# Graph attention layer: softmax denominators summed per node by matmuls instead of scanned per edge

## The reference

```
h = layernorm(feat);  fh, ft, fe = h @ W_head.T, h @ W_tail.T, h @ W_ent.T
e = einsum(leaky_relu(fh[src] * ft[dst]), attn) * log(deg)[dst] / 16     # one score per edge and head
ex = exp(e - segment_max(e, dst)[dst])
a = ex / segment_sum(ex, dst)[dst]
f = fe
for _ in range(5):
    f = 0.85 * segment_sum(f[src] * a, dst) + 0.15 * fe
```

## Time and profile before

| what | us |
|---|---|
| median of 3 runs | 7686.8 |
| lowest and highest run | 7684.38, 7687.97 |
| span of the profiled execution, first to last instruction | 6856.9 |
| median less span | 829.9 |
| VectorE alone on the softmax, 1444.5 to 1646.4 | 201.9 |
| hop 0, first matmul to last (1678.7 to 1985.3) | 306.6 |

### The profile page before, as it was taken

The page is one execution under the profiler, slowest core; times in us unless marked ns, Lnnn a source line. Parts: engine busy times, 40 slices in busy tenths (PEclk is TensorE's granted clock), DMA queues, the critical chain, the costliest instruction groups (busy, mean ns, idle before and its releaser), DMA issues.

```text
span 6856.9 us, 96632 instructions
## 1 busy us (share of the span) xinstructions
PE 4373.3 (64%) x19868; PEld 3745.1 (55%) x19869; DVE 3934.0 (57%) x8770; ACT 406.8 (6%) x1393; POOL 4142.0 (60%) x4109
## 2 busy tenths in 40 slices
PE   2754554632778888876666655666654666664899
PEld 1443443521668888865555544555543555543899
DVE  5764655677876666626666645666644666654211
ACT  0111111110000000000000000000000000001100
POOL 1477775721027777767777776777776777774000
PEclk9655555555985555555555555555555555555999
DMA  1344464511642222222222222222222222232576
GB/s 40 104 141 123 143 154 125 148 54 56 180 133 75 76 75 75 76 56 74 76 75 75 75 61 71 75 75 76 75 68 65 76 75 76 75 73 79 185 271 233
DMA packets 540070, 671.65 MB, mean 98 GB/s; under 512 B 102862, under 2 KB 425131, under 8 KB 529996
## 3 DMA queue, kind: packets, MB, share of 16 engines
q0 software_dynamic: 143584, 320.73, 17.3%
q1 hardware_dynamic: 396444, 350.42, 16.6%
HBM read 511.17 MB, written 160.80 MB: 98 GB/s over the span
## 4 chain that ended last, share of the span: by engine, by line
POOL 45%; issue 32%; PE 10%; DVE 7%; DMA 4%; SPq 2%; POOLq 0%; ACT 0%; DVEq 0%; ACTq 0%; PEldq 0%; PEld 0%
POOL U L676 45%; PE ps L1081 6%; DMA U<-edge_fe 2%; PE ps L868 1%; DVE U L1488 1%; DVE U L1460 1%; DVE U L1185 1%; SPq L542 1%; DVE U L1101 1%; DVE U L1504 1%; PE ps L944 1%; SPq L583 0%; DMA U<-tab_f,stage 0%; DVE U L1272 0%; PE ps L930 0%
## 5 line engine op out<-in xcount | busy, mean ns | idle before, releaser
L676 POOL DMA_INDIRECT U<-tab_f,stage x3224 | 3215.9, 997 | 1368.1 <-issue 979.4
L868 PE MATMUL ps<-U 128*125 128x128 f32 x8160 | 2126.4, 418 | 1277.6 <-DVE U L1185 1276.2
L868 PEld LDWEIGHTS ps<-U 128*125 128x125 f32 x8160 | 1725.3, 300 | 1489.6 <-issue 1489.6
L1125 DVE TENSOR_TENSOR U<-dloc,iota_p 128x500 f32<-128x500 f32 x1225 | 840.0, 686 | 1606.4 <-DMA U<-tab_f,stage 1541.7
L676 POOL DMA_INDIRECT U<-tab_he,stage x806 | 849.9, 1054 | 470.8 <-issue 239.0
L856 PE MATMUL ps<-gap 128*128 128x125 f32 x2816 | 828.1, 448 | 117.3 <-DVE gap L1148 64.6
L856 PEld LDWEIGHTS ps<-gap 128*128 128x128 f32 x2816 | 661.7, 325 | 276.6 <-DVE gap L1148 273.3
L1185 DVE TENSOR_TENSOR U<-U,ex_it 128x512 f32<-128x512 f32 x1020 | 705.6, 692 | 0.0
L969 PE MATMUL ps<-U 125*128 x1632 | 422.3, 440 | 215.7 <-ACT U L776 215.7
L865 PEld LDWEIGHTS ps<-w_it,U 128*125 128x125 f32 x1632 | 435.7, 327 | 213.0 <-issue 213.0
L1160 DVE SCALAR_TENSOR_TENSOR gap<-gap,U,ps 128x125 f32<-128x125 f32 x1408 | 483.8, 344 | 108.5 <-DVE gap L1160 18.3
(11 more groups left out here) (238 smaller groups left out, 2478.8 us busy)
## 6 DMA issues: line engine op xcount, KB each, us to landing
adj<-gap SPq DMA_DIRECT2D x1408, 64.0 KB
edge_fe<-U SPq DMA_DIRECT2D x204, 256.0 KB, 2.5
U<-edge_fe SPq DMA_DIRECT2D x204, 256.0 KB, 2.9
U<-tab_f,stage POOLq DMA_INDIRECT x3224, 2.6
ex_it<-adj SPq DMA_DIRECT2D x30, 1600.0 KB, 6.2
U<-adj SPq DMA_DIRECT2D x30, 1600.0 KB, 6.1
fe_a<-adj SPq DMA_DIRECT2D x15, 1600.0 KB, 6.2
U<-tab_he,stage POOLq DMA_INDIRECT x806, 3.1
```

The source lines that it names most:

```text
L676: pool.indirect_dma_start(to[:, k, j, :], None, table, bass.IndirectOffsetOnAxis(ap=stage[:, k, j:j + 1], axis=0)).then_inc(got[k], 16)
L868: mm = nc.tensor.matmul(ps[0:BN, bass.ds(b * F, F)], hot[:, k, j, :], ga[:, k, j, :], start=False, stop=False, skip_group_check=True)
L1125: return v.tensor_tensor(to[:, (k + ahead) % SLOTS], dloc[:, bass.ds(item_of(r, k, ahead), G)].unsqueeze(2).to_broadcast([P, G, BN]), iota ...
```

## The change

The exponentials are no longer divided edge by edge. The two summing scans, the mask, the reciprocals and the scaling of all edges go away; `ex_it` holds bare exponentials, and the transposes wait for `exps_ready` of the three parts. In hop 0 each item gets a second matmul with the same one-hot weight and 8 moving columns (`ex_it` of the item), which adds the exponentials of a node and head in PSUM behind the other sums (`EXP_SUMS`). At the end of hop 0 VectorE makes `share` = 0.85 / sum per node and head (200 values to a partition), every eviction of every hop multiplies the bank by `share`, in hop 0 followed by an add of `fe_a`; `fe_a` is then divided by `share` once, and in hops 1 to 4 TensorE starts each cleared bank with `ident` times that `fe_a`, seven more matmuls a hop, so that the eviction needs no add.

```diff
-SCANS = 4
+SCANS = 2
...
                         for j, b in enumerate(buckets):
+                            if s == 0:
+                                nc.tensor.matmul(ps[0:BN, bass.ds(b * HEADS + EXP_SUMS, HEADS)], hot[:, k, j, :],
+                                                 ex_it[:, bass.ds(r * PER_ITER + (k * G + j), 1), :].rearrange("p i h -> p (i h)"),
+                                                 start=False, stop=False, skip_group_check=True)
...
-                pe.wait_ge(shares_ready, -(-min(CI, (n + 1) * BPB) * EXP_PARTS // CI))
+                pe.wait_ge(exps_ready, -(-min(CI, (n + 1) * BPB) * EXP_PARTS // CI))
...
                 clear(range(BANKS))
+                if n:
+                    pe.wait_ge(share_ready, 1)
+                    for k in range(BANKS):
+                        b0, b1 = bank_buckets(k)
+                        nc.tensor.matmul(bank(k, (b1 - b0) * F)[0:BN], ident[0:BN, 0:BN],
+                                         fe_a[0:BN, b0:b1, :].rearrange("p b f -> p (b f)"),
+                                         start=False, stop=False, skip_group_check=True)
                 sum_pass(n)
...
-            link(v.tensor_scalar(bw, gap[:, 0:L], 0.0, None, ALU.is_equal))
-            dve.wait_ge(exps_ready, EXP_PARTS)
-
-            scan_carried(2, fw, bw, e_sc, fw[:, L - 1:L], False, summing=True)
-            scan_carried(3, bw[:, ::-1], gap[:, 1:L + 1][:, ::-1], fw[:, ::-1], bw[:, 0:1], True)
-            for part_ in parts:
-                link(v.reciprocal(bw[:, part_], bw[:, part_]))
-                v.scalar_tensor_tensor(out=e_sc[:, part_], in0=e_sc[:, part_], scalar=1.0 - ALPHA, in1=bw[:, part_],
-                                       op0=ALU.mult, op1=ALU.mult).then_inc(shares_ready, 1)
...
+                if n == 0:
+
+                    share_ = share[0:BN].rearrange("p b h -> p (b h)")
+                    link(v.tensor_scalar(share_, ps[0:BN, EXP_SUMS:EXP_SUMS + NB * HEADS], 1.0, None, ALU.max))
+                    link(v.reciprocal(share_, share_))
+                    link(v.tensor_scalar(share_, share_, 1.0 - ALPHA, None, ALU.mult))
                 for k in range(BANKS):
                     b0, b1 = bank_buckets(k)
-                    v.tensor_tensor(na[0:BN, b0:b1], bank(k, (b1 - b0) * F)[0:BN].rearrange("p (b f) -> p b f", f=F),
-                                    fe_a[0:BN, b0:b1], ALU.add).then_inc(sums_out, 1)
+                    to = na[0:BN, b0:b1].rearrange("p b (h d) -> p (b h) d", h=HEADS)
+                    ins = v.tensor_tensor(to, bank(k, (b1 - b0) * F)[0:BN].rearrange("p (n d) -> p n d", d=HD),
+                                          over_heads(b0, b1), ALU.mult)
+                    if n == 0:
+                        link(ins)
+                        ins = v.tensor_tensor(na[0:BN, b0:b1], na[0:BN, b0:b1], fe_a[0:BN, b0:b1], ALU.add)
+                    ins.then_inc(sums_out, 1)
                 dve.wait_ge(sums_out, (n + 1) * BANKS)
+                if n == 0:
+
+                    link(v.reciprocal(back[0:BN], share[0:BN].rearrange("p b h -> p (b h)")))
+                    fe_ = fe_a[0:BN].rearrange("p b (h d) -> p (b h) d", h=HEADS)
+                    v.tensor_tensor(fe_, fe_, back[0:BN].unsqueeze(2).to_broadcast([BN, NB * HEADS, HD]),
+                                    ALU.mult).then_inc(share_ready, 1)
```

More of the change, by code:

```diff
@@ L94 @@
 W_SUMS = (NB + 1) * F
+EXP_SUMS = (NB + 1) * F
 MASKS = 9
 assert PER_ITER == CHUNKS and ITEMS % CHUNKS == 0 and CHUNKS * HEADS == P and NB * BN == N_NODES
-assert W_SUMS + NB + 1 <= BANKS * BANK and BANKS < 8
+assert W_SUMS + NB + 1 <= BANKS * BANK and BANKS < 8 and EXP_SUMS + (NB + 1) * HEADS <= BANKS * BANK
 def bank_buckets(k):
@@ L198, in gnn_stack @@
         carry = sb("carry", [1, 5, HEADS * CHUNKS])
-        carry_col = sb("carry_col", [P, 4])
+        carry_col = sb("carry_col", [P, SCANS])
+        share = sb("share", [P, NB, HEADS])
         U = sb("U", [P, 3 * L])
@@ L409, in gnn_stack @@
         exps_ready = sem("exps_ready")
-        shares_ready = sem("shares_ready")
+        share_ready = sem("share_ready")
         exp_turned = sem("exp_turned")
@@ L1453, in _, with scan_carried @@
             dve.wait_ge(score_out, -(-CI // BPB))
[L1455 to L1460, removed]
+            def scan_carried(n, to, gaps, data, last, back):
+                link(v.tensor_tensor_scan(to, gaps, data, -BIG, ALU.add, ALU.max))
                 v.tensor_copy(ends[:, 0:1], last).then_inc(ends_ready, 1)
@@ L1469, in scan_carried @@
                 link(v.memset(carry[0:1, 3, :], 1.0))
-                link(v.memset(carry[0:1, 0:2, :], none))
+                link(v.memset(carry[0:1, 0:2, :], -BIG))
                 tt(cut[:, :, 1:], first[:, :, 1:], last_[:, :, :-1], ALU.not_equal)
@@ L1474, in scan_carried @@
                                             in1=gate[:, :, :-1], op0=ALU.mult, op1=ALU.add))
-                if summing:
-                    link(v.tensor_scalar(gates[:, :, 1:], gates[:, :, 1:], 0.0, None, ALU.is_equal))
                 link(v.tensor_copy(new[:, :, 1:], final[:, :, :-1]))
-                link(v.tensor_tensor_scan(carry[0:1, 2, :], carry[0:1, 0, :], carry[0:1, 1, :], none, *ops))
+                link(v.tensor_tensor_scan(carry[0:1, 2, :], carry[0:1, 0, :], carry[0:1, 1, :], -BIG, ALU.add, ALU.max))
                 to_col = carry[0:1, 4, :].rearrange("o (c h) -> o h c", h=HEADS)[:, :, way]
[L1480 to L1485, removed]
+                v.scalar_tensor_tensor(out=to_col, in0=cut, scalar=-BIG, in1=run, op0=ALU.mult,
+                                       op1=ALU.add).then_inc(carry_ready, 1)
                 dve.wait_ge(carry_turned, n + 1)
                 link(v.tensor_copy(carry_col[:, n:n + 1], bank(0, 1)))
-                link(v.tensor_tensor_scan(to, gaps, data, carry_col[:, n:n + 1], *ops))
+                link(v.tensor_tensor_scan(to, gaps, data, carry_col[:, n:n + 1], ALU.add, ALU.max))
             scan_carried(0, fw, gap[:, 0:L], e_sc, fw[:, L - 1:L], False)
@@ L1513, in _, with over_heads @@
             dve.sem_inc(acc_ready, 1)
+            back = grp_hot[:].rearrange("p a b -> p (a b)")[:, 0:NB * HEADS]
+            def over_heads(b0, b1):
+                return share[0:BN, b0:b1, :].rearrange("p b h -> p (b h)").unsqueeze(2).to_broadcast(
+                    [BN, (b1 - b0) * HEADS, HD])
             for n in range(HOPS):
```

## The result

The changed kernel takes 7953.81 us (median of 4 runs, 7946.24 to 7957.76), the kernel before 7686.33 us beside it (4 runs, 7684.38 to 7687.97). The ratio is 1.0342, 95% interval 1.033 to 1.0355: 267.5 us slower, where the prediction had 275.

What follows compares the result with a forecast made beforehand. It took VectorE alone to bound the softmax, and hop 0 to pass from VectorE to TensorE at 1.2 GHz; -119 + 391 + 3 = +275 us on 7686.8 gave 7962 us, range 7890 to 8005 at 0.8.

Steps and rivals of the forecast that it cites:

- The softmax: Before hop 0: transposes start after the first exponential, copies end near 1527.5 instead of 1646.43, 119 us earlier (118 to 120).
- Hop 0: 816 added narrow matmuls at 0.41 us make a group 3.4 us instead of 1.458: +391 us (+383 to +420).
- The ring: Hop 0's four group slots of load, VectorE and TensorE: 8.1 us a turn against 13.6, so TensorE alone paces.
- The clock: Hop 0's TensorE clock: expected to stay at 1.2 GHz (0.50) throughout, instead of today's 2.4 GHz.
- The 8.00 us row: Profile stretch 2900.2 to 2908.2 in hop 1: TensorE busy 8.00 of 8.00 us on such a mix, still at 0.50.
- The boundary: Between hop 0 and hop 1: new VectorE operations before the first bank's write add 2.6 us, taken as +3.
- The preload: Seven matmuls starting the banks of hops 1 to 4: 11 us a hop, hidden, cost 0; uncovered, 3 x 11 us.
- The sum: Whole kernel: -119 softmax, +391 hop 0, +3 boundary make +275 us, time 7962.
- The rival of the full clock: Hop 0 at 2.4 GHz: 1.82 to 2.06 us a group, time 7645 to 7693, break-even 2.035; chance 0.10.
- then it ends near no change: Sign that the forecast is wrong: hop 0 shows a granted clock of 1.00, and the time ends near today's.
- The 829.9 us: Gap between the kernel before's profiled span of 6856.9 us and its median, kept unchanged in the forecast.

Runs made afterwards that it cites:

- the fast chip: Changed kernel, code unaltered, run beside the kernel before on a chip of the faster kind: 7133.64 us against 6870.67.
- the bf16 form: Changed kernel with hop 0's narrow matmul in bf16 and all hops' messages scaled by the same cut exponentials: 7892.2 us, ratio 1.0134 to the kernel before.
- the twin: Changed kernel with hop 0's narrow matmul replaced by a second 128-column message matmul, sums left out: 7735.51 us, ratio 0.9922 to the kernel before.
- the padded kernel: Changed kernel with the eight exponentials followed by 120 zeros, copied by ScalarE, sums in their own bank: 6825.83 us against 6866.08 for the kernel before.
- the dense block: Changed kernel with six 512-column f32 matmuls put on TensorE after hop 0's third loop turn: 7122.67 us, ratio 1.0372 to the kernel before.

## Why the prediction was right

**The softmax: held.** Predicted 119 us off; 202.0 to 82.2 is 119.8. The transposes start on the first exponential and VectorE's 7.73 us of copies end the stage, as written.

**Hop 0: held, in size and in cause.** Predicted +391 us; measured 338.8 to 727.5, +388.7, on the fast chip. Three runs part it: without the narrow matmuls it is gone (336.5 us), with them and the scans both it is there alone (+387.3), and doubled they cost 0.416 us each, where 0.41 was taken. The ring, the load and VectorE set nothing: TensorE was busy for all of 675, 640 and 980 us.

**The clock: held.** This was the step that decided the size. 0.50 through hop 0 in the changed kernel, in the bf16 form, with the scans kept and with the narrow one doubled. The 8.00 us row was a good witness: a fully busy stretch of the mix with no rise. The Trainium skill (TensorE: Matmul & The Clock Gate, "Why this matters for your kernels") says that a TensorE kept continuously busy gets its full clock; the runs here disagree for this mix, with 640.00 of 640.00 us busy at 0.50, and agree for pairs of wide matmuls, 330.00 of 330.00 at 1.00. That the width of the added matmul decides is what the twin and the padded kernel point to: both have 128 columns in it, as many matmuls and weight loads as the changed kernel, and the clock at 1.00. But both also have its right operand at a fixed address, where the changed kernel takes it from the loop's register (the padded one has ScalarE's copies and a bank besides). No run has eight columns at a fixed address or 128 at one from the register, so the two are not parted, and why either should matter to the clock is open.

**The boundary: held.** +2.6 us was predicted from a 0.35, a 1.35 and a 0.25 us instruction and an add. They took 0.37, 1.40, 0.26 and 0.69; the gathers of hop 1 start 21.5 us after hop 0's last matmul, as against 18.8, so +2.7. The preload is hidden, shown by the run without it. Its size was off: 11 us predicted, 8.43 measured, since the clock rose within it (0.50 up to 2287.4 us of the fast chip's profile, 1.00 from 2288.0 on). The cover was therefore some 5 us and not 1.

**The sum.** -119.8 + 388.7 + 2.7 = 271.6 in the stages that the change touches. Measured were +263.0 us on the fast chip and +267.5 on the other. Hops 1 to 3 took 8.2 us less in the changed kernel's profile than in that of before (3214.5 to 3222.7), but these are single executions, perhaps on two chips, and I don't put that down to the change.

**The rival of the full clock: a term was missing from its price.** 1.82 to 2.06 us a group had been worked out by scaling the narrow matmul like the wide one. For TensorE's own passes that was about right: 1.75 right behind the dense block. The pace that followed was 2.27, and 2.26 with bf16 sums, so something other than the passes set it, and the rival had no term for that. With 2.27 hop 0 would grow by (2.27 - 1.458) x 201 = 163 us, and the kernel would be 163 - 119 + 3 = 47 us slower. That is an estimate from 16 us of one profile, and by it this form of the change loses even at 2.4 GHz: "then it ends near no change" was some 50 us off, and the one side that had spoken for faster was not there. What is missing may lie in TensorE's own queue. The trace of the run with the block has 12 register operations a group there, at the two matmuls' lines, those of the narrow one mostly of 0.08 us; the padded kernel has 8 and takes 1.87 us a group, the twin has 4 and takes 330 / 189 = 1.75 (VectorE's 378 instructions in its row are 189 groups). That this is the cause is argued, not shown.

**The 829.9 us: put in the wrong place.** The prediction had them between span and median. They are between two chips, as far as can be told: where the kernel takes 7811.42 us its span is 7809.5, and a span of 6856.9 fits the chips where it takes 6870. Nothing hung on it, as they stand on both sides of the difference; on the fast chip the span came out at 7135.0, for 7132 predicted.

**Expectations that missed.** I had the clock come back with the bf16 sums. It did not, so "a larger share of wide columns" is too simple a reading, or the share was still too small; no run here tells which. The rival written beside it, 2.6 us a group and about 104 us more than before, came true (101.8). The twin was to take 0.48 us an item and end between 26 us faster and 14 slower than before; it took 0.44 and was 54.9 faster. The kernel with the scans kept was to be 375 to 395 us slower and was 400.9, with hop 0 inside that range; the one with two narrow matmuls was to be about 595 slower and was 620.6, of which hop 0 explains 9 us. In these two some 10 to 14 us lie outside the stages looked at.

## What to carry to other kernels

Before adding matmuls to a stretch, price them by the spacing of weight loads in a row of the same mix, not by their columns, and then ask what they do to TensorE's clock: here eight columns cost 0.41 us, nearly what 128 cost at the same clock, and the lower clock took each wide one beside them from 0.24 to 0.44 us. If the clock is down beside a narrow matmul, try padding it with zeros to the width of its neighbours, from a buffer at a fixed address: with sixteen times the columns the pair took half the time. At the high clock look for a pace that the matmuls themselves don't explain, as the 2.27 us a group here. Moving work from an engine that is alone on the path (120 us of VectorE) to one at 78% in another stage is a gain only if the receiving stage still has the room at the clock it will then have.

## What the runs showed of the hardware

- The same mix of an f32 matmul with 8 columns and one with 128, each with its own weights, kept TensorE at 1.2 GHz for all of a 675 us stretch at 100% busy; two with 128 columns kept it at 2.4 GHz for 330 us. Raised by six dense matmuls, the clock lasted about 30 us into the narrow mix, in two kernels, and then stayed at 1.2 GHz to the end of hop 0. In all the mixes that stayed low the narrow matmul's right operand had an address from a register besides.
- At the low clock a pair of a narrow and a wide f32 matmul takes 0.84 us with one column in the narrow one and 0.85 with eight; a further narrow one costs 0.42 us, a bf16 one 0.21. At the high clock the pair with eight columns took 0.44 us where nothing held it up.
- With four such pairs to a group, each at an address from a register, a group took 2.26 to 2.27 us at the high clock, whether the narrow matmuls were f32 or bf16.
- Chips differ by 14% for one kernel: about 6870 us on two of them, 7686, 7790 and 7814 us in the other comparisons. Softmax and hop 0 agree to 2 us between them; each of hops 1 to 3, which gather, takes 1070 to 1076 us on the one kind and 1231 to 1277 on the other, over all the runs, where ScalarE and VectorE wait for something that the profile calls "remote". What that is, these runs leave open.
